# Softmax row sums over pairs of key tiles on the diagonal too, and the W2 butterflies among the projections

## The chip, the core and the metric

The kernel runs on one core of a Trainium2 chip. The metric is the device time of one execution in microseconds (us), the median of several runs. TensorE (PE) does the matmuls, VectorE (DVE), ScalarE (ACT) and GpSimd (POOL) work on tiles in SBUF and on PSUM banks, SyncE (SP) issues transfers. POOL can issue transfers too.

## What is computed

Two layers, each an attention part and a feed-forward part with a gated residual; only the first half of layer 0 is touched. Cut to that:

```python
h = _layernorm(x) * (1 + ca) + sa            # x is 2048 x 512
qkv = h @ W_qkv + b_qkv                      # 16 heads of 32
scores = einsum('bhqd,bhkd->bhqk', q, k) / sqrt(32)
scores = where(causal, scores, -10000.0)
ctx = einsum('bhqk,bhkd->bhqd', softmax(scores), v)
x = x + ga * (ctx @ W_out + b_out)
...
hidden = fwht(silu(h @ W1.T) * (h @ W3.T))   # Walsh-Hadamard over 2048
out = einsum('bsh,dh->bsd', hidden, W2)
```

The Walsh-Hadamard transform is its own transpose, so it can be applied to W2 instead of to the hidden values: four rounds of sums and differences (butterflies) over the 16 blocks of 128 rows of W2, the rest by a matmul later.

## The kernel before

**Projections** (`qkv_...`). The tokens go in four blocks of 512. Each block is 12 items (`PER`): 8 for queries and keys (m 0 to 7) and 4 for values (m 8 to 11), each of 12 matmuls of 128x512, high and low parts apart. For a query or key item ACT writes the high part to `out_hi` (L602), DVE the low part to `out_lo` (L670), and POOL issues a store for each (L501, L503) to the DRAM tensors q_hi, q_lo, k_hi, k_lo. Both buffers have two slots: item e waits for the landed stores of item e-2. Among the items stand parts of the next block: at m 1 its statistics, at m 3 its z (L155, DVE), and at m 5 its transposes (L166, PE), the scaling (L182, ACT) and the low half (L195, DVE), which pass each other two-slot tiles. The first twenty items also carry a step of the modulation vectors, in which PE waits for a copy by ACT. From item 30 on, score maxima are interleaved: PE writes a bank (L418), DVE reduces it (L446), two banks in turn. All engines run their instructions in the written order.

**Attention** (`attend_...`). 4 groups of 4 heads, 4 query blocks of 512 each: 16 units n = 4g + j. A unit walks 2(j+1) steps i, each over two key tiles of 128 keys: 80 steps. The first 2j steps of a unit lie off the diagonal, the last two on it; there a tile has only columns from 0, 128, 256 and 384 on. A step on PE: four score matmuls for one tile (L840), maxima of later units in between (L418), then the weighted values of the step before (L880, bank 6), then four scores more. ACT takes the exponential into `probs`, a ring of four tiles (L917). The row sums go to bank 7 by a matmul with ones (32 columns for each head). Off the diagonal POOL first adds the two tiles of a step (`add_pair`, L797) into one of two pair buffers, and PE sums the pair two steps later (`sum_pair`, L860). On the diagonal PE sums each tile by itself (L891). One pair buffer is the early half of `early_weights`, which carries the next stage's weights outside of attention.

**Butterflies.** W2 is taken in 8 slices of 64 columns (`fw`, two buffers in tokens_b). POOL loads a slice (L777, `load_columns`) at the start of units 0, 1, 2, 4, 5, 6, 8 and 9, and does its 8 instructions of 128x512 (L786, L787) and its store (L789) when it comes to the diagonal of that unit. At the start of attention POOL also sets ones and rows of the key tiles (L801, L804).

At the end of attention SP waits for the last pair sum and loads W_out and a gate row for the output projection (L91, L92).

Of the kernel before, what the change touches and what calls it, by code (L numbers as in the profile page):

```python
# [19 lines left out]
P = 128  # L20
S = 2048
D = 512
# [16 lines left out]
def build_program(nc, a, out):  # L39

    with ExitStack() as whole:
# [174 lines left out]
        with ExitStack() as ctx:  # L216
# [91 lines left out]
            fw = [tokens_b[:, 6144 + 1024 * i:7168 + 1024 * i].rearrange("p (c d) -> p c d", c=H0 // P)  # L308
# [26 lines left out]

            def off_before(n):
                g, j = divmod(n, NB)
                return g * (NB * (NB - 1)) + j * (j - 1)
# [51 lines left out]
            def off_index(s):  # L390
                n, i = steps[s]
                return off_before(n) + i
# [97 lines left out]
            def qkv_gpsimd(pool):  # L490
                for e in range(NB * 2 * G):
# [229 lines left out]
            def attend_sync(sp):  # L721
# [42 lines left out]
                sp.wait_ge(pairs_used, off_before(NQ))  # L764
# [3 lines left out]
            def attend_gpsimd(pool):  # L768

                w2 = a["w2t"].rearrange("(c p) d -> p c d", p=P)  # L770
                w2m = w2_mixed.rearrange("(c p) d -> p c d", p=P)

                def load_columns(s):
                    cols = slice(FW * s, FW * s + FW)
                    if s:
                        pool.wait_ge(fw_stored, 16 * s)
                    pool.dma_start(fw[0], w2[:, :, cols]).then_inc(fw_loaded, 16)  # L777

                def butterflies(s):
                    cols = slice(FW * s, FW * s + FW)  # L780
                    pool.wait_ge(fw_loaded, 16 * (s + 1))
                    for r in range(4):
                        half = 1 << r
                        src = fw[r % 2].rearrange("p (a b h) d -> p a b (h d)", b=2, h=half)
                        dst = fw[1 - r % 2].rearrange("p (a b h) d -> p a b (h d)", b=2, h=half)
                        nc.gpsimd.tensor_tensor(dst[:, :, 0, :], src[:, :, 0, :], src[:, :, 1, :], ALU.add).then_inc(fw_step, 1)  # L786
                        nc.gpsimd.tensor_tensor(dst[:, :, 1, :], src[:, :, 0, :], src[:, :, 1, :], ALU.subtract).then_inc(fw_step, 1)  # L787
                        pool.wait_ge(fw_step, 8 * s + 2 * r + 2)
                    pool.dma_start(w2m[:, :, cols], fw[0]).then_inc(fw_stored, 16)  # L789

                def add_pair(s):
                    o = off_index(s)
                    if o >= 2:
                        pool.wait_ge(pairs_used, o - 1)
                    for h in range(4):
                        pool.wait_ge(exp_done, 4 * (2 * s + 1) + h + 1)
                        nc.gpsimd.tensor_tensor(pairs[o % 2][:, h, :], probs[:, 2 * s % PS, h, :],  # L797
                                                probs[:, (2 * s + 1) % PS, h, :], ALU.add).then_inc(pair_ready, 1)
# [7 lines left out]
                mixed_at = {n: s for s, n in enumerate((0, 1, 2, 4, 5, 6, 8, 9))}  # L806
                for s, (n, i) in enumerate(steps):
                    if i == 0 and n in mixed_at:
                        load_columns(mixed_at[n])
                    if off_diagonal(s):  # L810
                        add_pair(s)
                    elif i == 2 * (n % NB) and n in mixed_at:
                        butterflies(mixed_at[n])
                pool.wait_ge(fw_stored, 16 * (D // FW))

            def attend_tensor(pe):
# [38 lines left out]
                def sum_pair(s):  # L855
                    n, i = steps[s]
                    o = off_index(s)
                    pe.wait_ge(pair_ready, 4 * (o + 1))
                    for h in range(4):
                        mm = nc.tensor.matmul(bank[7][HD * h:HD * h + HD, :], ones[:], pairs[o % 2][:, h, :],  # L860
                                              start=(i == 0), stop=False)
                    mm.then_inc(pairs_used, 1)

                def context(s):
# [6 lines left out]
                    elif i == 0:  # L871
                        pe.wait_ge(max_read, PRELUDE)
                        pe.wait_ge(ones_ready, 3)
                    for half in range(2):
# [8 lines left out]
                        if not diagonal:  # L883
                            mm.then_inc(probs_read, 1)
                    if not diagonal:
                        return
                    for half in range(2):
                        q, kt = 2 * s + half, 2 * i + half
                        c0 = first_column(n, kt)
                        for h in range(4):  # L890
                            mm = nc.tensor.matmul(bank[7][HD * h:HD * h + HD, c0:512], ones[:],  # L891
                                                  probs[:, q % PS, h, c0:512], start=(kt == 0),
                                                  stop=(last and half == 1))
                        mm.then_inc(probs_read, 1)

# [9 lines left out]
            def attend_scalar(act):  # L905
                for s, (n, i) in enumerate(steps):
                    for half in range(2):
                        q = 2 * s + half
                        c0 = P * max(2 * i + half - TB * (n % NB), 0)
                        for h in range(4):  # L910
# [4 lines left out]
                            if q >= PS and off_diagonal(s - 2):  # L915
                                act.wait_ge(pair_ready, 4 * off_index(s - 2) + h + 1)
# [3 lines left out]
            def attend_vector(dve):  # L920
# [4 lines left out]
                def finalize(n, part):  # L925
# [3 lines left out]
                    if part == 0:  # L929
                        dve.wait_ge(probs_read, quads_before(n + 1))  # L930
                        nc.vector.transpose(tile, bank[7][:]).then_inc(fin_step, 1)
# [6 lines left out]
                    else:  # L938
                        dve.wait_ge(fin_step, 3 * n + 3)
                        if n == 3 * NB:  # L940
                            dve.wait_ge(fw_stored, 16 * (D // FW))
# [944 lines left out]
```

## Time and profile before

| what | us |
|---|---|
| median of 3 runs | 2087.24 (2083.95 to 2090.82) |
| the profiled execution | 2086.4, span 2084.5 |
| projections, first item to last | about 24 to 210 |
| attention, up to the last row sum | about 210 to 793 |
| PE busy in the span | 1964.7 (94%) |
| DVE, ACT, POOL busy | 1078.9, 639.0, 439.6 |

A row of the timeline gives start, duration, engine, line, operation and, in brackets, the idle time before it and what ended that. A group row gives busy time, the mean of one instruction, and idle time before them. A float32 matmul stands in the trace as two records; four matmuls of 32 columns run side by side.

### The profile page before, as it was taken

The numbers are of one execution on the slowest core, as the hardware profiler recorded it, in microseconds if no ns is written. First come the engines' busy times: TensorE is split into PE (matmuls) and PEld (weight loads), VectorE is DVE, ScalarE is ACT, GpSimd is POOL, SyncE is SP. The second block draws the span as 40 slices with busy tenths as digits, with TensorE's granted clock in tenths as the row PEclk, the third lists the DMA queues.
The fourth block names the chain that finished last, engine by engine and source line by source line (L and its number), as shares of the span: only waits on it lengthen the run. The fifth ranks groups of instructions, "written<-read, shape, count | busy, mean of one in ns | idle before, by whom it ended". The sixth has DMA issues, their size and how long they took to land. (4 is left out here: it accounts for less than half of the span.)

```text
span 2084.5 us, 25631 instructions
## 1 busy us (share of the span) xinstructions
PE 1964.7 (94%) x10088; PEld 1399.4 (67%) x10088; DVE 1078.9 (52%) x1876; ACT 639.0 (31%) x1152; POOL 439.6 (21%) x385
## 2 busy tenths in 40 slices
PE   6999999999999997699999999997998969999998
PEld 4677545554545545578888888886885658888886
DVE  4456876666766715743434434336335665434334
ACT  3231445455555563322111111113221231111111
POOL 0122766666544365000000000000003000000000
PEclk9999999999999999899999999999999989999999
DMA  9753421422421003020000000002000011100002
GB/s 316 227 154 115 93 52 42 93 56 49 108 47 29 5 2 132 23 74 31 31 1 31 31 31 1 1 1 89 6 6 31 1 41 41 31 21 21 6 0 81
DMA packets 61720, 111.86 MB, mean 54 GB/s; under 512 B 6000, under 2 KB 21248, under 8 KB 61568
## 3 DMA queue, kind: packets, MB, share of 16 engines
q1 hardware_dynamic: 54144, 85.05, 14.2%
q0 software_dynamic: 7456, 25.18, 4.0%
q8 instruction: 80, 1.31, 0.3%
q14 instruction: 40, 0.33, 0.1%
HBM read 84.77 MB, written 25.44 MB: 53 GB/s over the span
## 5 line engine op out<-in xcount | busy, mean ns | idle before, releaser
L446 DVE TENSOR_REDUCE part_max<-banks 128x1 f32<-128x512 f32 (+2 forms) x640 | 357.3, 613 | 156.4 <-PE banks L418 96.6
L917 ACT ACTIVATE probs<-banks 128x512 f32<-128x512 f32 (+3 forms) x640 | 310.7, 538 | 282.7 <-PE banks L844 141.1
L418 PE MATMUL banks<-kst,qst 96*128 96x512 f32 (+2 forms) x640 | 261.6, 417 | 12.1 <-DVE part_max L446 9.2
L840 PE MATMUL banks<-qst,kst 98*128 98x512 f32 (+2 forms) x640 | 251.7, 413 | 0.2 <-ACT probs L917 0.2
L1384 DVE TENSOR_TENSOR tokens_a<-banks,tokens_a 128x512 f32<-128x512 f32 x224 | 151.5, 688 | 73.5 <-PE banks L210 71.9
L1409 DVE TENSOR_TENSOR tokens_b<-banks,tokens_b 128x512 f32<-128x512 f32 x64 | 44.3, 692 | 267.6 <-ACT tokens_b L1330 267.6
L208 PE MATMUL banks<-h_hi,f_wg_hi 128*128 128x512 f32 x432 | 170.4, 394 | 12.4 <-DVE f_wg_lo L1348 12.4
L208 PE MATMUL banks<-f_d_hi,f_hid_hi 128*128 128x512 f32 x432 | 171.7, 398 | 5.9 <-issue 3.6
L209 PE MATMUL banks<-h_lo,f_wg_hi 128*128 128x512 f32 x432 | 170.1, 394 | 0.0
L210 PE MATMUL banks<-f_d_hi,f_hid_lo 128*128 128x512 f32 x432 | 169.9, 393 | 0.0
L210 PE MATMUL banks<-h_hi,f_wg_lo 128*128 128x512 f32 x432 | 169.7, 393 | 0.0
L209 PE MATMUL banks<-f_d_lo,f_hid_hi 128*128 128x512 f32 x432 | 169.7, 393 | 0.0
L210 PE MATMUL banks<-h_hi,f_wu_lo 128*128 128x512 f32 x432 | 168.2, 389 | 0.0
L209 PE MATMUL banks<-h_lo,f_wu_hi 128*128 128x512 f32 x432 | 168.1, 389 | 0.0
L208 PE MATMUL banks<-h_hi,f_wu_hi 128*128 128x512 f32 x432 | 168.1, 389 | 0.0
L840 PEld LDWEIGHTS banks<-qst,kst 98*128 98x128 f32 x640 | 123.5, 194 | 63.5 <-issue 48.9
L1330 ACT ACTIVATE tokens_b<-banks 128x512 f32<-128x512 f32 x64 | 38.4, 600 | 413.7 <-PE banks L210 413.7
L418 PEld LDWEIGHTS banks<-kst,qst 96*128 96x128 f32 x640 | 123.6, 194 | 59.7 <-DVE part_max L446 45.7
L797 POOL TENSOR_TENSOR early_weights<-probs 128x512 f32<-128x512 f32 x96 | 122.5, 1310 | 120.4 <-ACT probs L917 120.3
L880 PE MATMUL banks<-probs,tokens_a 128*32 128x512 f32 (+3 forms) x1280 | 136.6, 545 | 0.5 <-DVE tokens_b L942 0.5
L797 POOL TENSOR_TENSOR pairs_own<-probs 128x512 f32<-128x512 f32 x96 | 120.1, 1285 | 56.0 <-ACT probs L917 56.0
L1548 POOL TENSOR_TENSOR w_lo<-early_weights,w_hi 128x512 fp32r<-128x512 f32 x4 | 5.1, 1308 | 592.6 <-ACT w_hi L1602 592.6
(188 smaller groups left out, 3268.7 us busy)
## 6 DMA issues: line engine op xcount, KB each, us to landing
tokens_a<-in_L_wmod SPq DMA_DIRECT2D x12, 1024.0 KB, 7.1
qst<-q_hi SPq DMA_DIRECT2D x32, 256.0 KB, 6.0
kst<-k_hi SPq DMA_DIRECT2D x32, 256.0 KB, 8.1
x<-in_L_attn_x SPq DMA_DIRECT2D x4, 1024.0 KB, 13.2
q_hi<-qk_out_hi POOLq DMA_DIRECT2D x16, 256.0 KB, 3.0
q_lo<-qk_out_lo POOLq DMA_DIRECT2D x16, 256.0 KB, 3.4
k_hi<-qk_out_hi POOLq DMA_DIRECT2D x16, 256.0 KB, 4.1
k_lo<-qk_out_lo POOLq DMA_DIRECT2D x16, 256.0 KB, 4.4
```

The source lines that it names most:

```text
L208: nc.tensor.matmul(dst, lh, rh, start=(first and i == 0), stop=False)
L209: nc.tensor.matmul(dst, lh, rl, start=False, stop=False)
L210: mm = nc.tensor.matmul(dst, ll, rh, start=False, stop=(last and i == n - 1))
L418: mm = nc.tensor.matmul(dst[:, 0:wide], qst[n % QS][0:BIASROW, h, P * t:P * t + P], kst[(NB * g + c) % KS][0:BIASROW, h, 0:wide], start=Tr ...
L446: nc.vector.tensor_reduce(part_max[:, n % 2, ht, c:c + 1], max_bank(slot)[:, 0:wide], AX_X, ALU.max).then_inc(max_read, 1)
L797: nc.gpsimd.tensor_tensor(pairs[o % 2][:, h, :], probs[:, 2 * s % PS, h, :], probs[:, (2 * s + 1) % PS, h, :], ALU.add).then_inc(pair_read ...
L840: mm = nc.tensor.matmul(dst[:, c0:512], kst[ck % KS][0:BIASROW + 2, h, at:at + P], qst[n % QS][0:BIASROW + 2, h, c0:512], start=True, stop ...
L880: mm = nc.tensor.matmul(bank[6][HD * h:HD * h + HD, c0:512], v[:, kt, at:at + HD], probs[:, q % PS, h, c0:512], start=(kt == 0), stop=(las ...
L917: nc.scalar.activation(probs[:, q % PS, h, c0:512], score_bank(sh)[:, c0:512], ACT.Exp, scale=SCALE).then_inc(exp_done, 1)
L1330: nc.scalar.activation(silu[:, u % 2, :], bank[2 * (u % 2)][:], ACT.Silu, scale=1.0 if mixed else gs[:, ch:ch + 1]).then_inc(silu_s, 1)
L1384: nc.vector.tensor_tensor(xt, bank[4 + n % 3][:], xt, ALU.add).then_inc(x_added, 1)
L1409: nc.vector.tensor_tensor(act_[:, u % 2, :], up_bank, silu[:, u % 2, :], ALU.mult).then_inc(hid_s, 1)
```

## The change

Row sums: nearly every diagonal step is now paired as well. For such a step PE sums the first tile's own 128 columns alone (`narrow_sums`), and POOL adds the two tiles over the columns that both have (`c0` from `pair_column`: 384 columns at i = 2j, 128 at i = 2j+1), which PE sums right behind the weighted values of the same step. Only the first step of units 0, 4, 8 and 12 stays as it was, since it opens the bank. `probs_read` is given after the weighted values and the narrow sum; ACT, before it overwrites a tile of `probs`, waits for the pair of two steps earlier, diagonal ones too; DVE's finalize waits for the last pair of its unit.

Butterflies: they leave attention. From item e = 4 of the projections on, POOL does one sum behind each high store and one difference behind each low store; four items make a slice, seven slices end with item 31, the eighth follows behind it without items between. Slice and next load go from `finish_columns`. The buffers are now the two halves of `early_weights`, in turn, which hold the values' weights until `w_ready` and the pair buffer from the first pair on.

```diff
-            fw = [tokens_b[:, 6144 + 1024 * i:7168 + 1024 * i].rearrange(...)
+            fw = [early[:, FW * (H0 // P) * i:FW * (H0 // P) * (i + 1)].rearrange(...)
...
+            pair_index = {}
+            for s, (n, i) in enumerate(steps):
+                if off_diagonal(s) or n % NB or i:
+                    pair_index[s] = len(pair_index)
+
+            def pair_column(s):
                 n, i = steps[s]
-                return off_before(n) + i
+                return P * max(2 * i + 1 - TB * (n % NB), 0)
...
             def qkv_gpsimd(pool):
...
+                def load_columns(c):
+                    if c == 0:
+                        pool.wait_ge(w_ready, KT + 2)
+                    pool.dma_start(fw[c % 2], w2[:, :, FW * c:FW * c + FW]).then_inc(fw_loaded, 16)
+
+                def butterfly(c, r, odd):
+                    if r == odd == 0:
+                        pool.wait_ge(fw_loaded, 16 * (c + 1))
+                        if c:
+                            pool.wait_ge(fw_stored, 16 * c)
+                    if odd == 0:
+                        pool.wait_ge(fw_step, 8 * c + 2 * r)
...
+                    nc.gpsimd.tensor_tensor(dst[:, :, odd, :], src[:, :, 0, :], src[:, :, 1, :],
+                                            ALU.subtract if odd else ALU.add).then_inc(fw_step, 1)
+
+                def finish_columns(c):
+                    pool.wait_ge(fw_step, 8 * c + 8)
+                    pool.dma_start(w2m[:, :, FW * c:FW * c + FW], fw[c % 2]).then_inc(fw_stored, 16)
+                    if c + 1 < SLICES:
+                        load_columns(c + 1)
...
                     pool.dma_start(hi[m % G, :, cols], ...)
+                    c, r = divmod(e - 4, 4)
+                    if c >= 0:
+                        butterfly(c, r, 0)
                     pool.wait_ge(qk_lo_ready, e + 1)
                     pool.dma_start(lo[m % G, :, cols], ...)
+                    if c >= 0:
+                        butterfly(c, r, 1)
+                        if r == 3:
+                            finish_columns(c)
+                    elif r == 3:
+                        load_columns(0)
+                for r in range(4):
+                    butterfly(SLICES - 1, r, 0)
+                    butterfly(SLICES - 1, r, 1)
+                finish_columns(SLICES - 1)
...
-                sp.wait_ge(pairs_used, off_before(NQ))
+                sp.wait_ge(pairs_used, len(pair_index))
                 sp.wait_ge(ctx_done, NQ - 1)
                 load_early_projection(sp, a["w_out0"], 0)
...
-                        nc.gpsimd.tensor_tensor(pairs[o % 2][:, h, :], probs[:, 2 * s % PS, h, :],
-                                                probs[:, (2 * s + 1) % PS, h, :], ALU.add)
+                        nc.gpsimd.tensor_tensor(pairs[o % 2][:, h, c0:512], probs[:, 2 * s % PS, h, c0:512],
+                                                probs[:, (2 * s + 1) % PS, h, c0:512], ALU.add)
...
+                def narrow_sums(s):
+                    n, i = steps[s]
+                    at = first_column(n, 2 * i)
+                    for h in range(4):
+                        mm = nc.tensor.matmul(bank[7][HD * h:HD * h + HD, at:at + P], ones[:],
+                                              probs[:, 2 * s % PS, h, at:at + P], start=False, stop=False)
+                    return mm
...
-                            if q >= PS and off_diagonal(s - 2):
-                                act.wait_ge(pair_ready, 4 * off_index(s - 2) + h + 1)
+                            if s - 2 in pair_index:
+                                act.wait_ge(pair_ready, 4 * pair_index[s - 2] + h + 1)
...
                         dve.wait_ge(probs_read, quads_before(n + 1))
+                        dve.wait_ge(pairs_used, pair_index[steps.index((n, 2 * j + 1))] + 1)
```

POOL's instructions in the first block of the projections, items 6 and 7 (stores k_hi, k_lo) and item 8 (q_hi, q_lo), before:

```order
L501 DMA k_hi<-qk_out_hi 128x512
L503 DMA k_lo<-qk_out_lo 128x512
L501 DMA k_hi<-qk_out_hi 128x512
L503 DMA k_lo<-qk_out_lo 128x512
L501 DMA q_hi<-qk_out_hi 128x512
L503 DMA q_lo<-qk_out_lo 128x512
```

This order is the same before and after for the stores. The same engine after the change, items 6 and 7 and the start of item 8 (`w_mixed` is the store of a slice, `in_w2t` the load of the next):

```order
L529 DMA k_hi<-qk_out_hi 128x512
L511 TENSOR_TENSOR early_weights<-early_weights 128x2x256
L534 DMA k_lo<-qk_out_lo 128x512
L511 TENSOR_TENSOR early_weights<-early_weights 128x2x256
L529 DMA k_hi<-qk_out_hi 128x512
L511 TENSOR_TENSOR early_weights<-early_weights 128x512
L534 DMA k_lo<-qk_out_lo 128x512
L511 TENSOR_TENSOR early_weights<-early_weights 128x512
L516 DMA w_mixed<-early_weights 128x16x64
L499 DMA early_weights<-in_w2t 128x16x64
L529 DMA q_hi<-qk_out_hi 128x512
L511 TENSOR_TENSOR early_weights<-early_weights 128x8x64
```

Each store now has an addition behind it, and the first addition of a slice stands ahead of a low store. PE in the last two steps of attention (unit 15, i = 6 and 7; the four scores between them are left out), before:

```order
L880 MATMUL banks<-probs,tokens_a 32x512 x4
L880 MATMUL banks<-probs,tokens_a 32x384 x4
L891 MATMUL banks<-probs,ones 32x512 x4
L891 MATMUL banks<-probs,ones 32x384 x4
...
L880 MATMUL banks<-probs,tokens_a 32x256 x4
L880 MATMUL banks<-probs,tokens_a 32x128 x4
L891 MATMUL banks<-probs,ones 32x256 x4
L891 MATMUL banks<-probs,ones 32x128 x4
```

And after the change:

```order
L895 MATMUL banks<-probs,tokens_a 32x512 x4
L918 MATMUL banks<-probs,ones 32x128 x4
L895 MATMUL banks<-probs,tokens_a 32x384 x4
L874 MATMUL banks<-early_weights,ones 32x384 x4
...
L895 MATMUL banks<-probs,tokens_a 32x256 x4
L918 MATMUL banks<-probs,ones 32x128 x4
L895 MATMUL banks<-probs,tokens_a 32x128 x4
L874 MATMUL banks<-pairs_own,ones 32x128 x4
```

The sums of 1280 columns have become sums of 768, and the last of each step reads what POOL has just added.

## Rows read from the trace of the kernel before

**Rows 1.** Windows: PE, PEld, DVE, ACT, POOL busy; clock, DMA share, GB/s.
```profile
165.00:210.00 45.00, 45.00 (x211) 34.12 (x210) 30.39 (x52) 6.79 (x9) 9.14 (x17) 1.00 0.26 95
...
210.00:735.00 525.00, 513.42 (x3460) 265.18 (x3458) 365.15 (x690) 272.82 (x556) 313.29 (x249) 0.98 0.26 57
```

**Rows 2.** Waits of PE between 210 and 735 us: total, times, longest.
```profile
PE banks L418 <- DVE part_max L446: 8.0, 21, 0.5
```

**Rows 3.** Groups by shape, PE: two records per matmul, four heads to a set.
```profile
L891 PE MATMUL banks<-probs,ones 128*32 128x512 f32 x128 | 16.7, 592 | 0.0
...
L891 PE MATMUL banks<-probs,ones 128*32 128x128 f32 x128 | 6.4, 273 | 0.0
...
L860 PE MATMUL banks<-early_weights,ones 128*32 128x512 f32 x192 | 25.6, 605 | 0.2 <-POOL early_weights L797 0.2
```

**Rows 4.** Groups by shape, POOL: busy us, mean ns of one.
```profile
L797 POOL TENSOR_TENSOR early_weights<-probs 128x512 f32<-128x512 f32 x96 | 122.5, 1310 | 120.4 <-ACT probs L917 120.3
...
L786 POOL TENSOR_TENSOR tokens_b<-tokens_b 128x512 f32<-128x512 f32 x32 | 40.8, 1275 | 16.2 <-DMA tokens_b<-in_w2t 14.3
...
L789 POOL DMA_DIRECT2D w_mixed<-tokens_b x8 | 9.4, 1174 | 4.6 <-POOL tokens_b L787 2.7 <-issue 1.9
...
L777 POOL DMA_DIRECT2D tokens_b<-in_w2t x8 | 9.3, 1166 | 27.5 <-DMA w_mixed<-tokens_b 27.2 <-POOL kst L804 0.3
...
L804 POOL MEMSET kst<- 2x2048 f32 x5 | 9.0, 1800 | 0.3
```

**Rows 5.** Landing of the W2 loads (line 777), then of the low stores (503).
```profile
DMA to landing us min/median/max: 5.7/6.0/12.7
...
DMA to landing us min/median/max: 2.6/4.0/8.3
```

**Rows 6.** Timeline of ACT, third block of the projections.
```profile
132.08 0.69 ACT L602 ACTIVATE qk_out_hi<-banks,qk_bias 128x512 fp32r<-128x512 f32 x1 [2.03 <-PE banks L210]
...
134.80 0.69 ACT L602 ACTIVATE qk_out_hi<-banks,qk_bias 128x512 fp32r<-128x512 f32 x1 [2.03 <-PE banks L210]
...
140.38 0.69 ACT L602 ACTIVATE qk_out_hi<-banks,qk_bias 128x512 fp32r<-128x512 f32 x1 [2.16 <-DMA q_lo<-qk_out_lo]
```

**Rows 7.** Timeline of PE, same block: the two places where it waits.
```profile
144.37 1.33 PE L166 MATMUL banks<-ident,n_z 128*128 128x128 f32 x8 [0.57 <-ACT n_h L182]
...
150.85 0.44 PE L418 MATMUL banks<-kst,qst 96*128 96x384 f32 x1 [1.16 <-DVE part_max L446]
```

**Rows 8.** Timelines of POOL, then DVE, in the output projection of layer 0.
```profile
805.31 23.59 POOL L1040 TENSOR_TENSOR tokens_a<-tokens_a,o_bias 128x512 f32<-128x512 f32 x16 [18.91 <-DVE o_bias L1034]
...
822.49 5.28 DVE L155 TENSOR_SCALAR n_z<-tokens_a,n_mv,n_rstd 128x512 f32<-128x512 f32 x4
...
841.24 1.92 DVE L155 TENSOR_SCALAR n_z<-tokens_a,n_mv,n_rstd 128x512 f32<-128x512 f32 x4
```

**Rows 9.** Timelines of POOL, then PE, from projections into attention.
```profile
195.09 0.54 POOL L503 DMA_DIRECT2D k_lo<-qk_out_lo  x1 [0.30 <-DVEq L674]
...
198.69 0.54 POOL L503 DMA_DIRECT2D k_lo<-qk_out_lo  x1 [0.30 <-DVEq L674]
...
211.24 0.13 POOL L801 MEMSET ones<- 128x32 f32 x1 [11.51 <-DVE tokens_a L679]
...
223.06 1.71 PE L880 MATMUL banks<-probs,tokens_a 128*32 128x512 f32 x16
```

**Rows 10.** The end of attention: POOL, PE, SP, DVE timelines, then a DMA row.
```profile
781.39 5.02 POOL L797 TENSOR_TENSOR pairs_own<-probs 128x512 f32<-128x512 f32 x4
...
789.10 1.69 PE L891 MATMUL banks<-probs,ones 128*32 128x512 f32 x16
...
787.84 0.40 SPq L91 DMA_DIRECT2D early_weights<-in_w_out  x1
...
799.39 1.29 DVE L1029 TENSOR_TENSOR early_weights<-early_weights,early_gate 128x512 f32<-128x512 f32 x2
...
early_gate<-gates SPq DMA_DIRECT2D x2, 256.0 KB, 7.0
```

More of the change, by code:

```diff
@@ L307, in build_program @@
             FW = 64
-            fw = [tokens_b[:, 6144 + 1024 * i:7168 + 1024 * i].rearrange("p (c d) -> p c d", c=H0 // P)
+            fw = [early[:, FW * (H0 // P) * i:FW * (H0 // P) * (i + 1)].rearrange("p (c d) -> p c d", c=H0 // P)
                   for i in range(2)]
@@ L490, in qkv_gpsimd @@
             def qkv_gpsimd(pool):
+                w2 = a["w2t"].rearrange("(c p) d -> p c d", p=P)
+                w2m = w2_mixed.rearrange("(c p) d -> p c d", p=P)
+                SLICES = D // FW
+                def load_columns(c):
[9 more added lines that the diff above has]
+                        pool.wait_ge(fw_step, 8 * c + 2 * r)
+                    half = 1 << r
+                    src = fw[(c + r) % 2].rearrange("p (a b h) d -> p a b (h d)", b=2, h=half)
+                    dst = fw[(c + r + 1) % 2].rearrange("p (a b h) d -> p a b (h d)", b=2, h=half)
+                    nc.gpsimd.tensor_tensor(dst[:, :, odd, :], src[:, :, 0, :], src[:, :, 1, :],
[5 more added lines that the diff above has]
+                        load_columns(c + 1)
                 for e in range(NB * 2 * G):
@@ L768, in attend_gpsimd @@
             def attend_gpsimd(pool):
[L770 to L789, printed above, removed]
                 def add_pair(s):
-                    o = off_index(s)
+                    o, c0 = pair_index[s], pair_column(s)
+                    if o == 0:
+                        pool.wait_ge(fw_stored, 16 * (D // FW))
                     if o >= 2:
@@ L796, in add_pair @@
                         pool.wait_ge(exp_done, 4 * (2 * s + 1) + h + 1)
-                        nc.gpsimd.tensor_tensor(pairs[o % 2][:, h, :], probs[:, 2 * s % PS, h, :],
-                                                probs[:, (2 * s + 1) % PS, h, :], ALU.add).then_inc(pair_ready, 1)
+                        nc.gpsimd.tensor_tensor(pairs[o % 2][:, h, c0:512], probs[:, 2 * s % PS, h, c0:512],
+                                                probs[:, (2 * s + 1) % PS, h, c0:512], ALU.add).then_inc(pair_ready, 1)
                 pool.wait_ge(qkv_done, PER * NB)
@@ L805, in attend_gpsimd @@
                 pool.wait_ge(ones_ready, KS + 1)
[L806 to L814, printed above, removed]
+                for s in pair_index:
+                    add_pair(s)
             def attend_tensor(pe):
@@ L856, in sum_pair @@
                     n, i = steps[s]
-                    o = off_index(s)
+                    o, c0 = pair_index[s], pair_column(s)
                     pe.wait_ge(pair_ready, 4 * (o + 1))
                     for h in range(4):
-                        mm = nc.tensor.matmul(bank[7][HD * h:HD * h + HD, :], ones[:], pairs[o % 2][:, h, :],
-                                              start=(i == 0), stop=False)
+                        mm = nc.tensor.matmul(bank[7][HD * h:HD * h + HD, c0:512], ones[:], pairs[o % 2][:, h, c0:512],
+                                              start=(i == 0), stop=(i == 2 * (n % NB) + 1))
                     mm.then_inc(pairs_used, 1)
@@ L873, in context @@
                         pe.wait_ge(ones_ready, 3)
+                    paired = s in pair_index
                     for half in range(2):
@@ L882, in context @@
                                                   stop=(last and half == 1))
-                        if not diagonal:
+                        if paired:
+                            if diagonal and half == 0:
+                                mm = narrow_sums(s)
                             mm.then_inc(probs_read, 1)
-                    if not diagonal:
+                    if paired:
+                        if diagonal:
+                            sum_pair(s)
                         return
@@ L891, in context @@
                             mm = nc.tensor.matmul(bank[7][HD * h:HD * h + HD, c0:512], ones[:],
-                                                  probs[:, q % PS, h, c0:512], start=(kt == 0),
-                                                  stop=(last and half == 1))
+                                                  probs[:, q % PS, h, c0:512], start=(kt == 0), stop=False)
                         mm.then_inc(probs_read, 1)
+                def narrow_sums(s):
[5 more added lines that the diff above has]
+                    return mm
                 for s, (n, i) in enumerate(steps):
```

6 lines of the change are left out of this document (removed).

## The prediction

> **What bounds the kernel now.** I read the windows first, since the change touches two stretches with different limits. From 165 to 210 us, the last block of the projections, PE is busy 45.00 of 45 us; from 210 to 735, nearly all of attention, 513.42 of 525, and POOL 313.29 [rows 1]. So PE sets the time in both, and POOL's work is hidden. The waits of PE in attention say who could hold it: 8.0 us in 21 short waits for DVE's maxima, and for POOL only 0.2 us [rows 2, 3]. It follows that taking butterflies out of attention gains nothing by itself; there only fewer columns on PE count. The projections look as safe, with POOL at 9.14 of 45 us [rows 1], but there ACT and DVE hand PE its banks, and ACT already waited once for the landing of a low store (item 20, 2.16 us) [rows 6]. That is where POOL's queue reaches PE.
>
> **Fewer columns in attention.** A set of four heads at 512 columns is eight records, so the 128 records of line 891 are 16 sets, 16.7 us, 1.04 each; at 128 columns 6.4 / 16 = 0.40. The difference over 384 columns is 0.64 us, 1.68 ns a column; the rest is a tail that the next set covers [rows 3]. A unit with j > 0 has summed 512 + 384 + 256 + 128 = 1280 columns on the diagonal and will sum 128 + 384 + 128 + 128 = 768: 512 x 1.68 ns = 0.86 us, for twelve units 10.3 us. A unit with j = 0 saves 128 columns, 0.21 us, four of them 0.9. Number of sets and waits of PE stay, so 11.2 us is the gain if nothing follows. It can be as little as 0 if DVE's maxima are late next, but 8.0 us of such waits in 525 [rows 2] say that they seldom are; I take it nearly whole.
>
> **The new wait for pairs in attention.** PE now sums a diagonal pair right behind the weighted values of its step. An addition of 512 columns takes 1.31 us [rows 4]; 384 or 128 columns do not occur. Their bounds are 0 and 1.31; in proportion they are 0.98 and 0.33, and I take that. Four of 384 then take 3.9 us from the first exponential of the second tile on. While maxima stand between the scores, PE comes to the sum some 7 us after that exponential (a step lasts 7 to 9 us there: 80 steps in about 570 us, fewer than 5 us only at the end), so it waits nowhere before 735 us. In the last unit steps last 5 us and POOL has no air: its last pair off the diagonal starts at 781.39 and ends at 786.4, the new one would end at 790.3, and PE would be there at about 789.10 + 0.2 [rows 10]. One microsecond of wait takes back that unit's 0.86 us. Queued behind PE's wait are the four last scores, and for them wait ACT, the last 128-column pair and DVE's finalize. Gain in attention: 11.2 - 0.9 - 0.1 = **10.2 us**.
>
> **The load of W_out.** SP issued it at 787.84, when the last pair off the diagonal had been summed, 5.6 us before the end of attention; now it must wait for the last diagonal pair, at about 793.5. The gate row behind it lands 7.0 us after its issue, so at 794.0 + 7.0 = 801.0; DVE took it up at 799.39 [rows 10]. The loss is 1.6 us, between 0 (a quick landing) and 3.5: I take **1.7 us**.
>
> **Butterflies among the projections.** Per item POOL issues two stores (0.54 each [rows 9]) and does two additions (1.28 each [rows 4]): 3.7 us with the gaps. Items come every 2.72 us in the third block (132.08 to 134.80 [rows 6]) and every 3.60 in the fourth (195.09 to 198.69 [rows 9]). After four items come a store and a load (1.17 each [rows 4]), and the next slice's first sum waits until the load has landed, 6.0 us after its start [rows 5]; the low store of that item is queued behind it. The stores go by POOL's queue, ACT's item e+2 waits for item e's, and behind ACT wait PE's steps. Where a block begins, the four value items before it (no stores) give POOL time and the load is hidden. In the middle of a block it isn't: loads at items 4, 12, 20 and 28.
>
> Fourth block, worked out: let item 27's high store be ready at 0. Its low store and second addition end at 3.7, the slice's store at 4.9, where the load starts; it lands at 10.9; the sum of item 28 ends at 12.2, its low store lands 4.0 later [rows 5], at 16.2. ACT's item 30 was due 1 us ahead of its own store, at 3 x 3.6 - 1.0 = 9.8. It is 6.4 us late. DVE's low half waits for it, behind that stand DVE's maxima, and PE, which has two banks for them, already waited 1.16 us for DVE at such a place [rows 7]. There is no slack, so PE loses some 6.2 us.
>
> Third block, items 16 to 23: POOL falls behind by 1.0 us an item. At item 21 ACT is 3.9 us late through the landing of item 19's low store, and its scaling behind that is what PE's transposes wait for (0.57 us already [rows 7]): 3.6 us. Then the load at item 20 makes item 22 late, again with maxima behind: 4.2 us more. Second block: items 12 and 14 are late by 1.2 and 1.5 us, ahead of the copies that PE's modulation steps wait for: 2.5 us. First block: the load at item 4 makes item 6 late by 3 us, but that item stands behind ACT's scaling anyhow: 0. Sum 6.2 + 7.8 + 2.5 = **16.5 us**. The bounds: with landings at their least (5.7 and 2.6 [rows 5]) the same steps give about 11; with the load at 8 us instead of 6.0, 22; its greatest, 12.7 [rows 5], more.
>
> **The tail.** After item 31 POOL does the last slice without cover. Before, that item's low store was issued at 198.69; now, 16.5 us later and with its own lag, at about 217.6. Then the addition, store, load (lands at about 228), eight additions of 1.28, the store, the store of the gates and its landing: ones are set at about 241. They were ready at 211.24, and the first weighted values started at 223.06 [rows 9], which 16.5 us make 239.6. PE waits about **1.5 us**. The rows of the key tiles (1.80 each [rows 4]) are ready 9 us later, and unit 2 needs them 30 us later still.
>
> **DVE beside POOL.** While POOL ran sixteen additions back to back, four z instructions of DVE took 5.28 us, and when it had done, the same four took 1.92 [rows 8]. In the projections such instructions (z, the low halves) now meet additions that fill 2.6 of each 3.7 us; z feeds the transposes. 3.4 us could be lost in each of three blocks, but it overlaps with the lateness above: 0 to 8 us, I take **2 us**. The Trainium skill states this as a rule (SBUF — State Buffer, "Who interferes with whom"): DVE in a two-port mode, or with two inputs in SBUF, and a GpSimd instruction that reads SBUF exclude one another, and a reduction from PSUM does not contend. By that rule the butterflies are moved from a place without contention (attention's maxima) into one with it; the trace agrees, by 5.28 against 1.92 us.
>
> **Sum.** 2086.4 - 10.2 + 1.7 + 16.5 + 1.5 + 2 = 2097.9. The profiled execution lies 0.8 us below the median, so 2098.7: about 2099.
>
> **Rivals.** *The queue is harmless* (faster). If the 6.0 us of a load were mostly latency that falls in idle time, or ACT's and DVE's lead covered it, the projections would lose 4 us with all: 2087.2 - 10.2 + 1.7 + 4 = 2083, and down to 2079 with none. For it speaks that PE runs up to four items ahead in the first two blocks; against it that from item 30 on the maxima tie PE to DVE. It decides at a lateness of about 8.5 us in the projections; below that the kernel is faster. 0.14. *Transfers are crowded.* A load beside the x and modulation loads took up to 12.7 us [rows 5]; at 10 us for each of the three exposed loads instead of 6, 12 us more: 2111. 0.14. *The columns don't pay*: the small sets take as long as the large, or DVE's maxima are next: 2099 + 8 = 2107. 0.12. My forecast has 0.60, with its own range 2089 to 2108.
>
> **Range and chances.** 2084 to 2112 leaves out the lower half of the first rival, part of the second and little else. A measurement can tell about 0.3% here, 6.3 us, so faster is below 2081, slower above 2093.5. Faster: 0.08, a bit over half of the first rival. Same: the rest of it and the lower end of my own case, 0.20. Slower: 0.72.
>
> **What would show it.** In the projections: PE idle behind DVE or ACT at items 21, 22 and 30, ACT's waits for landings of q_lo and k_lo up from single microseconds, z near 1.3 us each. The first weighted values should start at about 241. From there to the end of attention it should take about 10 us less than 570. W_out should be issued at the very end of attention. I am wrong if the projections end within 8 us of before, or if PE waits for POOL on many diagonal steps.

## The result and the profile after

The changed kernel takes 2113.93 us (median of 4 runs, 2112.36 to 2115.24), the kernel before 2086.12 in the runs beside it: 1.013 times the time, interval 1.011 to 1.015. It is slower by 27.8 us; 12 were forecast, and 2113.9 lies above the range. The profiled executions have spans of 2111.4 and 2084.5 us, 26.9 apart. I cut each span at four places: the last matmul of the projections, the first weighted values of attention, its last row sum, and PE's next matmul. The first two cuts answer to [rows 9], the last two to [rows 10].

| stretch, us | before | after | difference |
|---|---|---|---|
| projections, up to | 210.4 | 242.8 | +32.4 |
| from there to the first weighted values | 12.7 | 16.4 | +3.7 |
| attention | 570.3 | 563.5 | -6.8 |
| last row sum to PE's next matmul | 8.2 | 8.3 | +0.1 |
| the rest | 1282.9 | 1280.4 | -2.5 |

In the rest nothing was changed; over all kernels here it lies between 1280.1 and 1284.5. So the projections decided it.

Windows of the kernel after (the columns of [rows 1]): all of the projections, the third block, their last 45 us as in [rows 1], and attention:

```profile
20.00:243.00 223.00, 189.19 (x860) 137.07 (x860) 133.03 (x195) 48.68 (x73) 127.42 (x138) 0.93 0.64 197
...
141.00:187.00 46.00, 32.02 (x137) 24.09 (x136) 24.28 (x41) 8.34 (x13) 34.92 (x37) 0.85 0.69 189
...
165.00:210.00 45.00, 37.56 (x170) 27.50 (x169) 24.27 (x44) 4.13 (x6) 32.46 (x34) 0.92 0.59 170
...
259.00:822.80 563.80, 549.38 (x3848) 283.33 (x3848) 354.37 (x671) 304.91 (x628) 326.70 (x310) 0.98 0.17 35
```

The same stretches of the kernel before:

```profile
20.00:210.50 190.50, 180.16 (x861) 131.30 (x860) 108.55 (x195) 48.63 (x73) 39.40 (x67) 0.99 0.58 189
...
223.00:793.40 570.40, 557.60 (x3849) 283.86 (x3848) 356.26 (x674) 304.81 (x628) 339.95 (x271) 0.99 0.23 52
```

The first row of each has the same 860 records of PE, but they are busy for 189.19 us and not 180.16: behind idle time PE works on at the lower of its two levels (1.2 instead of 2.4 GHz) for a while, and the granted clock is 0.93 instead of 0.99. While the lower level was granted, PE was busy for 20.4 us, before for 3.4; half of the 17 us between them is 8.5. So of the 32.4 us some 9 are a slower clock and 23 are idle time. In the third block PE is busy 32 of 46 us. Over all of the projections POOL's busy time goes from 39 to 127 us. In attention PE is busy 8.2 us less and idle 1.6 more.

PE's timeline in the third block (answering to [rows 7]) shows where more than half of the idle time lies:

```profile
157.01 3.96 PE L166 MATMUL banks<-ident,n_z 128*128 128x128 f32 x16 [6.53 <-DVE n_z L155]
...
175.07 0.58 PE L419 MATMUL banks<-kst,qst 96*128 96x256 f32 x1 [7.09 <-DVE part_max L447]
```

POOL's timeline at the same place:

```profile
153.94 1.27 POOL L511 TENSOR_TENSOR early_weights<-early_weights 128x512 f32<-128x512 f32 x1
155.51 1.21 POOL L516 DMA_DIRECT2D w_mixed<-early_weights  x1 [0.30 <-POOL early_weights L511]
156.72 1.16 POOL L499 DMA_DIRECT2D early_weights<-in_w2t  x1
157.87 0.56 POOL L529 DMA_DIRECT2D k_hi<-qk_out_hi  x1
167.92 1.25 POOL L511 TENSOR_TENSOR early_weights<-early_weights 128x512 f32<-128x512 f32 x1 [9.48 <-DMA early_weights<-in_w2t]
169.12 0.57 POOL L534 DMA_DIRECT2D k_lo<-qk_out_lo  x1
```

The low half of item 20 was ready at 157.6, so its store could have left right behind the high one, at 158.4; it left at 169.12, behind the wait for the load. ACT, which needs its buffer two items later, stood 9.36 us for its landing, and behind ACT stand DVE's maxima and PE (7.09). The other wait, 6.53 us, is for z. DVE's timeline, which answers to [rows 8]; it is the same four instructions that took 1.92 before:

```profile
150.77 6.18 DVE L155 TENSOR_SCALAR n_z<-x,n_mv,n_rstd 128x512 f32<-128x512 f32 x4
```

### The profile page after: what moved, and what is told of

Same layout as the page of the kernel before. It is cut to its first block and busy times, and to the rows that moved or that the text cites. A ratio compares the mean times of both kernels' runs of the same rounds, so it can differ in the third digit from the quotient of the medians.

```text
span 2111.4 us, 25950 instructions
## 1 busy us (share of the span) xinstructions
PE 1960.1 (93%) x10088; PEld 1401.8 (66%) x10088; DVE 1102.3 (52%) x1876; ACT 639.3 (30%) x1152; POOL 515.3 (24%) x497
## 3 DMA queue, kind: packets, MB, share of 16 engines
q8 instruction: 80, 1.31, 0.3%
## 5 line engine op out<-in xcount | busy, mean ns | idle before, releaser
L447 DVE TENSOR_REDUCE part_max<-banks 128x1 f32<-128x512 f32 (+2 forms) x640 | 357.1, 615 | 157.6 <-PE banks L419 93.1
L818 POOL TENSOR_TENSOR early_weights<-probs 128x512 f32<-128x512 f32 (+2 forms) x152 | 160.6, 1085 | 116.2 <-ACT probs L943 115.8
L818 POOL TENSOR_TENSOR pairs_own<-probs 128x512 f32<-128x512 f32 (+2 forms) x152 | 157.4, 1063 | 120.0 <-ACT probs L943 119.7
L208 PE MATMUL banks<-h_hi,f_wg_hi 128*128 128x512 f32 x432 | 170.4, 394 | 12.5 <-DVE f_wg_lo L1373 12.5
L895 PE MATMUL banks<-probs,tokens_a 128*32 128x512 f32 (+3 forms) x1280 | 143.0, 550 | 4.2 <-issue 3.6
```

Source lines behind the costliest of these rows:

```text
L208: nc.tensor.matmul(dst, lh, rh, start=(first and i == 0), stop=False)
L447: nc.vector.tensor_reduce(part_max[:, n % 2, ht, c:c + 1], max_bank(slot)[:, 0:wide], AX_X, ALU.max).then_inc(max_read, 1)
L818: nc.gpsimd.tensor_tensor(pairs[o % 2][:, h, c0:512], probs[:, 2 * s % PS, h, c0:512], probs[:, (2 * s + 1) % PS, h, c0:512], ALU.add).the ...
L895: mm = nc.tensor.matmul(bank[6][HD * h:HD * h + HD, c0:512], v[:, kt, at:at + HD], probs[:, q % PS, h, c0:512], start=(kt == 0), stop=(las ...
```

## The experiments

The same cuts through all kernels (profiled executions; "ratio" is against the kernel before, with its 95% interval):

| kernel | ratio | projections end | to first weighted values | attention |
|---|---|---|---|---|
| before | | 210.4 | 12.7 | 570.3 |
| after | 1.013 [1.011, 1.015] | 242.8 | 16.4 | 563.5 |
| e1_sums_only | 1.014 [1.013, 1.016] | 209.6 | 12.7 | 601.8 |
| e2_move_only | 1.017 [1.015, 1.019] | 244.3 | 16.4 | 573.5 |
| e3_stores_first | 1.013 [1.011, 1.015] | 243.1 | 17.4 | 560.7 |
| e4_no_additions | 1.001 [1.000, 1.003] | 225.9 | 12.7 | 561.8 |
| e5_additions_only | 1.007 [1.005, 1.008] | 230.1 | 12.7 | 560.3 |
| e6_writes_only | 1.004 [1.003, 1.005] | 230.8 | 13.1 | 562.0 |
| e7_spread | 0.999 [0.998, 1.000] | 210.5 | 12.7 | 567.4 |
| e9_pause | 1.001 [1.000, 1.002] | 211.2 | 12.7 | 570.0 |
| e11_earlier | 0.996 [0.994, 0.997] | 211.0 | 12.7 | 562.2 |

### The two halves of the change

**e1_sums_only**: only the row sums are changed. The butterflies stay in attention, eight in a row as before, behind the unit's last diagonal pair.

```diff
+                    if i == 2 * (n % NB) + 1 and n in mixed_at:
+                        butterflies(mixed_at[n])
```

> Only the row-sum half of the change; the butterflies stay in attention, behind the last diagonal pair of their units, with their old buffers. If the projections' queue is what cost the time, this one keeps only the gain: attention shorter by the 6.7 us seen in the changed kernel up to the 10 us of columns, 2076 to 2080 us. Rival, the new waits for POOL's diagonal pairs eat the columns: 2084 to 2088.

2115.77 us: neither number. The projections are as before, attention is 31 us longer. POOL's timeline from unit 1 into unit 2:

```profile
277.67 1.28 POOL L788 TENSOR_TENSOR tokens_b<-tokens_b 128x512 f32<-128x512 f32 x1
280.80 1.18 POOL L790 DMA_DIRECT2D w_mixed<-tokens_b  x1 [1.85 <-issue]
285.91 1.15 POOL L778 DMA_DIRECT2D tokens_b<-in_w2t  x1 [3.94 <-DMA w_mixed<-tokens_b]
287.08 4.93 POOL L798 TENSOR_TENSOR pairs_own<-probs 128x512 f32<-128x512 f32 x4
```

The additions end at 279, but the next unit's first pair starts at 287.08, behind the landing of the store and the issue of the load. Before, eight additions filled steps in which no pair was due; now a pair is due in nearly every step. PE's waits in attention say what it costs:

```profile
PE banks L841 <- ACT probs L930: 11.5, 6, 4.1
PE banks L419 <- DVE part_max L447: 8.2, 22, 0.5
PE banks L861 <- POOL early_weights L798: 6.6, 4, 2.3
PE banks L419 <- DMA kst<-k_hi: 5.4, 2, 3.3
PE banks L861 <- POOL pairs_own L798: 4.9, 4, 1.9
```

PE was idle 28 us more than before, and its mean granted clock in attention fell from 0.985 to 0.957. So the new sums don't pay with the butterflies eight in a row behind a unit's last pair. That gives the move a purpose that I had missed when I wrote that taking butterflies out of attention gains nothing.

**e2_move_only**: attention's code of before, the butterflies in the projections.

> Only the butterflies' half: attention as before, the additions and transfers among the projections' stores. If the two halves add, the projections end 32 us later, PE waits some 3.6 us more for the ones, and nothing is gained: 2118 to 2124 us. Rival, that the new row sums are part of the loss: below 2114.

2123.23 us, as expected. The projections lose 33.9 us with the row sums untouched, the start of attention 3.7. Attention is 3.2 us longer without its butterflies, not shorter: PE's idle time there is the same (12.4 us, before 12.8), its busy time is higher at a lower clock. So taking butterflies out of attention gained nothing by itself, as forecast.

### What in the projections

**e3_stores_first**: both stores of an item go ahead of both its additions.

```diff
-                    if c >= 0:
-                        butterfly(c, r, 0)
                     pool.wait_ge(qk_lo_ready, e + 1)
                     pool.dma_start(lo[m % G, :, cols], ...)
+                        butterfly(c, r, 0)
```

> The changed kernel, with both stores of an item ahead of its two additions. If the low store queued behind the load's landing is the cause, the load wait now falls on the next item's stores, later by one item (3.6 us): the three exposed loads cost 2 to 3 us less each, ACT's items become ready earlier, 2104 to 2109 us. If the additions cost time because they hold DVE up, their order matters little: 2111 to 2115.

2112.9 us: no gain clear of noise, as the second forecast had it. The item's low store no longer stands behind an addition or a load, but the next item's stores do. PE's waits for maxima behind the loads of the third and fourth block came to 12.2 us (13.9 in after), so each got shorter by under 1 us, not by 2 to 3. In the profiled execution PE was idle 3.5 us less than in after until the projections' end, but busy 3.8 us more, at a granted clock of 0.930 against 0.937.

**e4_no_additions**: stores, loads and their waits stay, the additions are left out (W2 goes untransformed).

```diff
-                    nc.gpsimd.tensor_tensor(...).then_inc(fw_step, 1)
+                    pool.sem_inc(fw_step, 1)
```

> The changed kernel without its 64 additions (the slices are loaded and stored as they are, so W2 is not transformed; this work is left out). What remains is the wait for loads ahead of low stores. If additions in the queue and in DVE's way are the larger part: projections some 6 to 9 us longer than before, 2084 to 2092 us in all. If the transfers and their landings are the cause: 2100 to 2108.

**e5_additions_only**: all 64 additions at their places, but only two loads at the start, and no slice stores, so POOL waits for a landing only once, ahead of its first addition. The additions' results are not used: W2 is copied untransformed.

> The changed kernel with its 64 additions among the projections' stores, but two loads instead of eight and no slice store there, so no addition waits for a landing (W2 is copied untransformed in attention; the transform is left out). Transfers alone made the projections 15.5 us longer. If the two causes add to 32.4, additions alone make them 17 us longer, 2093 to 2100 us in all. If each needs the other (additions only hurt once loads have made POOL late), under 10 us longer: 2083 to 2090.

2088.49 and 2099.87 us. The time of e4_no_additions lies in its first forecast, but its projections end 15.5 us later, not 6 to 9; e5_additions_only came out as the sum of two causes would have it. The projections lose 15.5 us by the transfers alone and 19.8 by the additions alone; together they lose 32.4, nearly the sum.

**e6_writes_only**: as after, but each addition is four memsets of 256 columns, 327 ns each, so 1.31 us in all: POOL is held as long and writes SBUF (1024 columns, where an addition writes 512), but reads nothing (transform left out). The lines below leave out a wait of each difference for its sum.

```diff
-                    nc.gpsimd.tensor_tensor(dst..., src..., src..., ...)
+                    for part in range(3):
+                        nc.gpsimd.memset(whole_dst[:, 4 * part:4 * part + 4, :], 0.0)
+                    nc.gpsimd.memset(whole_dst[:, 12:16, :], 0.0).then_inc(fw_step, 1)
```

> The changed kernel with each addition replaced by four settings of 256 columns to zero, about as long on GpSimd, which read nothing from SBUF (the transform is left out). All transfers and waits stay. If additions hurt by holding up DVE's instructions that use the same way into SBUF, z and the low halves are short again and the projections 4 to 10 us shorter than the changed kernel's: 2102 to 2109 us. If they hurt by standing in POOL's queue, as before: 2111 to 2115.

2092.58 us, 9 below the nearer forecast, so both missed the time; the projections end 20.4 us later in the profiled execution. POOL's queue holds the same stores behind the same lengths of work, and 12.0 of the 32.4 us are gone. Those belong to the additions' reading. But 12.0 is rather too little: each share is read from one profiled execution, and this one took 2100.25 us, 7.7 above the median of its eight; that of e4_no_additions lies 3.9 above its median. If I take each kernel's median against before, and from its profile only what attention and the stretches at its two ends changed, the projections lose 30.8 us in after, 8.2 in e4, 21.2 in e5 and 14.3 in e6 (an estimate). The reading then has 16.5 us, and the transfers less than their 15.5. The groups of DVE in the projections show on which instructions; columns as in [rows 3], first after:

```profile
L711 DVE SCALAR_TENSOR_TENSOR qk_out_lo<-banks,qk_bias,qk_out_hi 128x512 fp32r<-128x512 f32 x32 | 24.0, 750 | 58.7 <-ACT qk_out_hi L643 58.0 <-DVE qk_out_lo L711 0.7
L195 DVE TENSOR_TENSOR ht_lo<-n_h,ht_hi 128x512 fp32r<-128x512 f32 x16 | 16.4, 1027 | 8.5 <-ACT ht_hi L176 8.0
L155 DVE TENSOR_SCALAR n_z<-x,n_mv,n_rstd 128x512 f32<-128x512 f32 x12 | 14.8, 1290 | 0.1
...
L692 DVE SCALAR_TENSOR_TENSOR gate_rows<-const_stage,gate_size 128x512 f32<-128x512 f32 x4 | 9.1, 2271 | 0.1
...
L193 DVE CAST ht_hi<-n_h 128x512 fp32r<-128x512 f32 x8 | 6.9, 858 | 0.0
```

and e6_writes_only:

```profile
L195 DVE TENSOR_TENSOR ht_lo<-n_h,ht_hi 128x512 fp32r<-128x512 f32 x16 | 11.1, 692 | 7.9 <-ACT ht_hi L176 7.3
L155 DVE TENSOR_SCALAR n_z<-x,n_mv,n_rstd 128x512 f32<-128x512 f32 x12 | 10.6, 943 | 0.1
...
L193 DVE CAST ht_hi<-n_h 128x512 fp32r<-128x512 f32 x8 | 5.9, 738 | 0.0
L696 DVE SCALAR_TENSOR_TENSOR gate_rows<-const_stage,gate_size 128x512 f32<-128x512 f32 x4 | 2.8, 692 | 0.1
```

Mean ns of one, before / e4 / e6 / after: z 542 / 813 / 943 / 1290; the transposes' low halves (ht_lo) 692 / 692 / 692 / 1027; gate_rows (a step of the modulation vectors) 692 / 692 / 692 / 2271; the high halves of the transposes that DVE makes (line 193) 420 / 420 / 738 / 858; the low halves of queries and keys (qk_out_lo) 749 / 750 / 750 / 750.

How late the items of PE end against before shows at which places the 32.4 us were lost (profiled executions):

| lateness added, us | forecast | after | e4 | e5 | e6 |
|---|---|---|---|---|---|
| first block | 0 | 4.9 | 0.6 | 4.8 | 0.5 |
| second | 2.5 | 2.7 | 0.4 | 2.5 | 1.4 |
| third, and the fourth up to m 6 | 7.8 | 16.3 | 9.4 | 12.5 | 10.2 |
| fourth, from m 7 on | 6.2 | 8.5 | 5.1 | 0 | 8.3 |

The first two blocks are lost by the additions (e5 has nearly all of it, e4 little; e6 has little of the first and half of the second). The fourth is the landing of the load: e5, which waits for none there, loses nothing. The additions make it worse by 3.4 us (8.5 against 5.1), by their length in the queue, since e6 has 8.3. The third has both, and there they overlap: e4 and e5 lose 21.9 us together, after 16.3. So the two causes add up to nearly 32.4 only because an overlap in the third block and an extra loss in the fourth almost cancel.

### Another place for the butterflies

**e7_spread**: the new row sums, and the butterflies in attention in their old buffers, but one or two behind each pair instead of eight in a row. The next load is issued right behind a slice's store.

```diff
+                for s in range(len(steps)):
+                    if s in pair_index:
+                        add_pair(s)
+                    for _ in range(share(s)):   # 0 to 2
+                        if mixing:
+                            butterfly(*mixing.pop(0))
```

> The new row sums with the butterflies in attention, but one or two additions behind each pair instead of eight in a row behind a unit's diagonal, and the next slice's load issued as soon as its buffer is free. If the eight in a row made the sums-only kernel slow, attention is now as short as in the changed kernel and the projections as before: 2076 to 2081 us. If GpSimd has no room for both in attention: 2090 to 2115.

2084.63 us, between the two forecasts: the 32.4 and 3.7 us are gone, but attention takes 567.4 us, not the 561.8 of e4, which has no butterflies there. One place in POOL's timeline stands out:

```profile
273.00 1.15 POOL L777 DMA_DIRECT2D tokens_b<-in_w2t  x1
284.63 1.28 POOL L789 TENSOR_TENSOR tokens_b<-tokens_b 128x512 f32<-128x512 f32 x1 [10.48 <-ACT probs L943]
285.88 4.93 POOL L811 TENSOR_TENSOR pairs_own<-probs 128x512 f32<-128x512 f32 x4
```

The releaser named is ACT, but the first addition of a slice waits for its load (and the store ahead), issued at 271.8 and 273.0. The pair was queued behind it, and PE waited 3.2 us for pairs. That is less than the 5.6 us that are missing: PE is idle 3.0 us more than in e4 and busy 2.6 us more, at a clock of 0.979 against 0.985.

**e9_pause**: after a slice's store and load, two more pairs come before the next addition.

```diff
+                    if pause:
+                        pause -= 1
+                        continue
...
+                            if len(mixing) % 8 == 0:
+                                pause = 1
```

> Row sums as in the changed kernel, butterflies in attention as in e7_spread, one or two behind each pair; new is only that GpSimd, once it has issued a slice's store and the next load, adds two more pairs before the first sum of the new slice. My theory: what e7_spread lost against the attention of e4_no_additions (567.4 against 561.8 us) is one place, where the first sum of a slice stood ahead of the next pair and waited 10.5 us for the load to land; pairs were late for five steps after it, and PE waited 3.2 us for them. Then the attention should take 561 to 563 us here, PE should wait under 1 us for GpSimd's pairs, the projections should end at about 210 as before, and the time should be 2077 to 2081 against about 2086 before (ratio 0.996 to 0.998). Rival: the additions themselves slow attention wherever they stand (they read SBUF beside ACT's exponentials and DVE's maxima): then attention stays at 566 to 568 us and the time at 2083 to 2085.

2087.05 us: a miss on the time by both theories, though not on the mechanism. PE's waits for POOL fell to 1.3 us. But the last slice now ended later, and DVE ran into it. The row of PE's waits in attention:

```profile
PE banks L419 <- DVE part_max L447: 17.8, 23, 9.6
```

DVE's timeline, with what ended its idle time:

```profile
687.70 0.69 DVE L975 TENSOR_TENSOR tokens_b<-banks,early_gate 128x512 f32<-128x512 f32 x1 [9.34 <-DMA w_mixed<-tokens_b]
```

And POOL's, the last slice's store:

```profile
682.81 1.17 POOL L793 DMA_DIRECT2D w_mixed<-tokens_b  x1 [0.30 <-POOL tokens_b L789]
```

Unit 12's finalize writes over the buffers of the slices and waits for the last store to land.

**e11_earlier**: up to three additions instead of two where a step has a narrow pair or none.

```diff
-                        return 2
+                        return 3
```

> As e9_pause, but GpSimd does up to three butterfly additions instead of two behind a narrow pair (128 columns) and where a step has no pair, so that the last slice is stored some four steps earlier. In e9_pause the wait for a load no longer reached PE, but the last slice's store was issued at 682.81 us, and DVE's finalize of unit 12, which overwrites the buffer, waited 9.34 us for it; PE stood 9.62 us behind DVE's maxima. My theory: that wait is all that e9_pause lost; taken away, the attention takes 560 to 562 us (as long as in e4_no_additions, where it holds no butterflies), PE waits under 2 us for GpSimd's pairs, and the time is 2076 to 2079, some 8 us below before (ratio about 0.996). Rival: the butterflies cost attention something wherever they stand: attention stays at 566 us or above and the time at 2083 or above; in e9_pause and e7_spread two different waits would then have hidden the same loss.

2078.0 us, ratio 0.996 [0.994, 0.997]: 8.5 us below before and 36 below after. Attention takes 562.2 us, as in e4. The last slice's store leaves at 658.27, and PE's waits in attention are back:

```profile
PE banks L419 <- DVE part_max L447: 8.3, 23, 0.5
...
PE banks L880 <- POOL early_weights L811: 0.9, 1, 0.9
```

So the additions cost attention nothing as long as no pair and no finalize stands behind a landing. POOL is busy 414 of 562 us there.

## Why the prediction was wrong in size

- **What bounds the kernel** was right: PE, and in the projections POOL's queue reaches it through ACT and DVE.
- **Fewer columns**: the gain was forecast as 11.2 us, 10.2 after all deductions. The sums with ones went from 97.4 us in their groups (lines 860 and 891) to 87.3, so 10.1; the narrow set takes 0.40 us (224 records, 11.2 us) as forecast. But PE as a whole is busy only 8.2 less; the groups of weighted values rose by 1.4 us. What is missing is the clock, which was in no term. In after PE stands 3.64 us ahead of its first weighted values and starts them at the lower level (granted clock 0.50 from 257.2 to 264 us; before, 1.00 in the same place):

```profile
L895 PE MATMUL banks<-probs,tokens_a 128*32 128x384 f32 x128 | 14.0, 509 | 0.0
...
L910 PE MATMUL banks<-probs,ones 128*32 128x512 f32 x32 | 5.1, 709 | 0.0
```

  In e11_earlier, which has the same sums and starts attention without that wait, these groups take 13.3 and 4.2 us, the sums with ones 86.3 us in all (11.1 less than before), and PE is busy 10.1 us less in attention. So the size of this term was right at the full clock. Attention gained 6.8 us in after and 8.1 in e11_earlier.
- **The new wait for pairs**: right. PE waits 0.9 and 0.5 us in the last unit (forecast 0.9 and 0.1), nowhere else. An addition of 384 columns takes 1.02 us (0.98 taken), one of 128 takes 0.46 (0.33).
- **The load of W_out**: forecast +1.7, measured +0.1. It was issued at 822.79, at the very end as said. The 7.0 us of [rows 10] is the median of two loads, and the one at this place landed in 5.6 us in both kernels, after at 828.81. DVE took up the weights at 828.83, right behind the splitting of the context (line 1078), for which it had to wait in any case. A hiding step stood beside this load, and I had not looked for it.
- **Butterflies among the projections**: forecast 16.5 + 2, measured 32.4. This is the term that failed. The rate of POOL (3.6 us an item), the fourth block (6.2 against 8.5) and the second (2.5 against 2.7) were near. The first block was taken at nothing and cost 4.9, through DVE's stretched instructions (below). The third block was sized at 7.8 and cost 16.3. Its load landed not in 6.0 us but in 11, beside SP's loads of queries and keys for the maxima, so that the second wait is 7.09 instead of 4.2 us; this is the rival of crowded transfers, at one load and not at three. And the block's first wait is 6.53 us for z, not 3.6 for the scaling. The load of 12.7 us that the rival was priced by also stood beside SP's loads of queries and keys, in attention (issued at 271.18), not beside loads of x and modulation. Landings of the W2 loads here, 6.9 at least, answer to [rows 5]:

```profile
DMA to landing us min/median/max: 6.9/7.1/11.1
```

- **DVE beside POOL**: z was forecast at 1.3 us and took 1.29 in the mean. The error was to take it as 2 us of 0 to 8. The additions' reading cost 12.0 us by the profiles and 16.5 by the medians (the estimate above). Other kinds are stretched too, and each stands where somebody waits: in the first block gate_rows (2.13 us instead of 0.69) stands right ahead of a low half of the transposes (1.66 instead of 0.69), for which ACT's scaling waited 4.53 us, 2.12 before; for z PE itself waits. DVE's timeline there:

```profile
58.83 2.13 DVE L692 SCALAR_TENSOR_TENSOR gate_rows<-const_stage,gate_size 128x512 f32<-128x512 f32 x1
61.11 1.66 DVE L195 TENSOR_TENSOR ht_lo<-n_h,ht_hi 128x512 fp32r<-128x512 f32 x1
```

  "It overlaps with the lateness above" was the reason. But in the first two blocks, where the transfers alone cost 1.0 us (e4), there was little to overlap with, and in the third the reading still cost 6.1 us (16.3 against the 10.2 of e6). The Trainium skill (SBUF — State Buffer, "Who interferes with whom") says that a DVE instruction with two inputs in SBUF contends with a GpSimd instruction that reads SBUF, not with one that only writes. The trace agrees: ht_lo and gate_rows are at 692 ns in e4 and e6 and at 1027 and 2271 in after. I had named this rule, and the low halves under it, and then priced it by z alone.
- **The lower clock** was in no term. PE's busy time rose by 9.0 us at the same records, behind idle stretches that the change brought.
- **The tail**: forecast 1.5, measured 3.7. Load 7.0 instead of 6.0, 1.0 before the last slice's store, 3.4 for the landing of the gates.

Of the sign the prediction was right for its reason: a gain on PE in attention, a greater loss in the projections through POOL's queue. Left open is how the reading's share falls to z, the halves of the transposes and gate_rows; no run separates them. Nor was it tried to move the slice transfers to SP's queue.

## What to carry to other kernels

Work of a mostly idle engine is free only where nothing that others wait for is queued behind it; for each landing it waits for, name that work, and put independent pieces of it between a load's issue and its first use (two pairs were enough here). When work on GpSimd is moved, list every DVE instruction beside which it will run, by its inputs (two in SBUF, or one, as in z and the casts of line 193), and price each by who waits for it; do not price one and call the rest overlap. And add for each idle stretch that a change puts on TensorE the time at the lower clock behind it: here 9 us on 23 in the projections.

## What the runs showed of the hardware

- z (one input in SBUF) is stretched already when POOL only issues transfers (542 to 813 ns, e4), but only beside the issue of a slice's store or load, which holds POOL for 1.17 us (five of the twelve z, 1152 to 1240 ns); beside the issue of a low store it keeps its 540. Plain writes stretch it more (943, e6), and the cast of line 193 too (420 to 738). DVE instructions with two SBUF inputs are stretched only by POOL's reading; one that reads PSUM and SBUF (qk_out_lo) by nothing.
- An instruction with two SBUF inputs can be held longer than one addition lasts. In e5_additions_only a low half of 0.69 us took 3.62 while each addition of POOL takes 1.3:

```profile
158.09 3.62 DVE L195 TENSOR_TENSOR ht_lo<-n_h,ht_hi 128x512 fp32r<-128x512 f32 x1 [1.75 <-ACT ht_hi L176]
```

- POOL's additions showed no such stretch: 1293 ns in the projections, beside DVE, and 1275 in attention before [rows 4].
